# A vision tower with a mixture of experts on one core: the first steps in a new order of loads and set-up pieces, the first weight matrix with a semaphore of its own

## The reference

```python
gray = jnp.einsum('bchw,c->bhw', x, w)[:, None]
edges = conv(gray, scharr)                       # two 3x3 filters
edge = jnp.sqrt(jnp.square(edges)).sum(axis=1) / 2
h = concatenate([cls_tok row, edge rows])         # 257 rows
xn = layernorm(h)
u, v, q, k = split(silu(xn @ W1 + b1), 4)        # W1: 256 x 1024
attn = silu(q @ k.T per head) / S                # 16 heads of 16
h = h + (layernorm((attn @ v) * u) * gamma + beta) @ W2 + b2
h = h + ffn(layernorm(h))    # router: statistics, gelu, softmax, top 2 of 32
                             # experts with a capacity, 16 adjugates
```

## Time and profile before

| what | value |
|---|---|
| median of 3 runs | 1460.76 us |
| the profiled execution's own time | 1461.07 us |
| its span | 1459.2 us |
| TensorE busy | 1273.0 us, 87% |
| VectorE busy | 1212.3 us, 83% |
| ScalarE busy | 892.8 us, 61% |
| POOL busy | 482.5 us, 33% |
| mean granted TensorE clock | 0.932 of full speed |
| moved by DMA | 176.69 MB, mean 121 GB/s |

### The profile page before, as it was taken

How to read it: one execution, slowest core, us unless ns; L and a number is a source line. 1 busy time by engine, 2 the same in 40 slices (tenths; PEclk the granted TensorE clock), 3 DMA queues, 4 the chain that set the end, 5 groups by cost and what they waited for, 6 DMA issues and landing times. The chain is left out here.

```text
span 1459.2 us, 33138 instructions
## 1 busy us (share of the span) xinstructions
PE 1273.0 (87%) x11891; PEld 1025.1 (70%) x11891; DVE 1212.3 (83%) x3140; ACT 892.8 (61%) x1608; POOL 482.5 (33%) x457
## 2 busy tenths in 40 slices
PE   3699999999999999999973332499999999999996
PEld 2457667667667667667652232399999999999996
DVE  4589999999999999999879878877777777777773
ACT  1378878887887887887772352545555555555552
POOL 0022232233233233232213000235554545555543
PEclk9699999999999999999996555699999999999999
DMA  8535344345345445442040600055565665665652
GB/s 242 136 93 132 107 122 132 105 123 133 103 125 133 107 120 133 113 115 59 31 145 17 93 1 0 14 192 156 163 191 151 178 179 148 186 171 150 195 126 24
DMA packets 128185, 176.69 MB, mean 121 GB/s; under 512 B 19946, under 2 KB 116476, under 8 KB 123964
## 3 DMA queue, kind: packets, MB, share of 16 engines
q1 hardware_dynamic: 110652, 153.80, 35.6%
q0 software_dynamic: 17408, 21.25, 9.1%
HBM read 133.85 MB, written 41.15 MB: 120 GB/s over the span
## 5 line engine op out<-in xcount | busy, mean ns | idle before, releaser
L796 ACT ACTIVATE at<-ps_s 128x1024 f32<-128x1024 f32 x256 | 248.3, 1027 | 5.4 <-PE ps_s L532 4.3
L2368 POOL DMA_INDIRECT out_rows<-ye,slot_token x96 | 151.8, 1581 | 227.2 <-ACT ye L2213 213.5
L247 PE MATMUL ps_s<-xet,whi 128*128 128x322 f32 x640 | 206.1, 322 | 11.1 <-DVE wlo L2283 9.6
L249 PE MATMUL ps_s<-xet,whi 128*128 128x322 f32 x640 | 199.3, 311 | 0.0
L248 PE MATMUL ps_s<-xet,wlo 128*128 128x322 f32 x640 | 198.7, 310 | 0.0
L2182 ACT ACTIVATE sg<-ps_s 128x322 f32<-128x322 f32 x160 | 70.5, 440 | 172.5 <-PE ps_s L249 128.2
L2283 DVE TENSOR_TENSOR wlo<-raw,whi 128x640 fp32r<-128x640 f32 x192 | 153.9, 817 | 2.3 <-ACT whi L2192 1.3
L2266 DVE TENSOR_TENSOR hm<-ps_s,sg 128x322 f32<-128x322 f32 x128 | 63.2, 494 | 98.6 <-ACT sg L2182 77.6
L548 PE MATMUL ps_av<-at,uv 128*16 128x257 f32 x2048 | 136.8, 384 | 1.0 <-ACT at L840 0.5
L247 PEld LDWEIGHTS ps_s<-xet,whi 128*128 128x128 f32 x640 | 121.6, 190 | 19.3 <-issue 15.8
L247 PE MATMUL ps_av<-whi,hs 128*128 128x256 f32 (+1 forms) x480 | 134.5, 280 | 0.6 <-issue 0.3
(11 more groups left out here) (393 smaller groups left out, 3557.2 us busy)
## 6 DMA issues: line engine op xcount, KB each, us to landing
raw<-in_wexp SPq DMA_DIRECT2D x32, 1280.0 KB, 6.4
halo<-gray_dram SPq DMA_DIRECT2D x96, 288.0 KB
xb<-in_x SPq DMA_DIRECT2D x64, 384.0 KB, 4.8
raw<-in_wexp SPq DMA_DIRECT2D x32, 640.0 KB
gray_dram<-g SPq DMA_DIRECT2D x32, 256.0 KB, 3.5
out_rows<-h SPq DMA_DIRECT2D x64, 128.0 KB, 3.3
token_rows<-xf SPq DMA_DIRECT2D x64, 128.0 KB, 2.4
pre_dram<-pre SPq DMA_DIRECT2D x30, 128.0 KB, 1.7
```

Source lines behind the costliest of these rows:

```text
L247: nc.tensor.matmul(o, lh, rh, start=first, stop=False)
L249: return nc.tensor.matmul(o, lh, rl, start=False, stop=last)
L796: nc.scalar.activation(at[:, t, 2 * i:2 * i + 2, :, 0:R].rearrange("p j k q -> p (j k) q"), ps_s[i][:, :, :, :].rearrange("p j k q -> p (j ...
L2368: nc.gpsimd.indirect_dma_start(out=out, out_offset=bass.IndirectOffsetOnAxis(ap=slot_token[0:w, 3 * m + st:3 * m + st + 1], axis=0), in_=y ...
```

## The change

It touches the fill alone. SyncE's order is new: of the constants only the first 256 columns are loaded at the start (the rest, from the mask of the class values on, moves into the list of the later loads); the zeroing of `gray_dram` goes ahead of the taps and the class rows; W1 and b1qk follow, under the semaphore `w1_loaded`; then come the first gray's store, the pixels of image 1 and the first halo, and only then the other loads. On VectorE the cast of W1 becomes a piece of its own (`round_w1`), and the other pieces of the set-up move from step -2 into step -1, with the gray of image 2; the gray of image 3 goes to the end of step -1. TensorE and ScalarE follow with their own orders. The number of instructions stays the same but for one DMA.

```diff
--- before.py
+++ after.py
@@ -305,13 +305,14 @@
         fill = zeros[:, 0:3 * ROW].rearrange("p (n w) -> p n w", w=ROW)
         base_loaded, loaded, zeroed, filled, zero_set = (sem(n) for n in ("base_loaded", "loaded", "zeroed", "filled", "zero_set"))
         su_dve, su_act, su_pool, su_pe = sem("su_dve"), sem("su_act"), sem("su_pool"), sem("su_pe")
+        w1_loaded = sem("w1_loaded")
+        w1_group = [(w1f, w1.rearrange("(k p) n -> p k n", p=P)), (b1qk_sb[:, :], b1qk)]
         loads = [
-            (w1f, w1.rearrange("(k p) n -> p k n", p=P)), (gbf, gb), (b1qk_sb[:, :], b1qk),
-            (w2f, w2.rearrange("(k p) n -> p k n", p=P)), (r1f, r1w.rearrange("(k p) n -> p k n", p=P)), (r1mf, r1m), (b2f, b2),
+            (cst[:, CMV:NC_], consts[:, CMV:NC_]), (gbf, gb), (w2f, w2.rearrange("(k p) n -> p k n", p=P)), (r1f, r1w.rearrange("(k p) n -> p k n", p=P)), (r1mf, r1m), (b2f, b2),
             (b1uv_sb[:, :], b1uv), (r1b_c[:, :], r1b), (r2w_sb[:, :], r2w),
         ]
         LOADED = 16 * (len(loads) + 3)
-        S_BAND, S_VAR, S_CLSN, S_CLST, S_GAIN, S_W1, S_CW, S_W2, S_UVP, S_BIAS, S_R1, S_VC, S_ALL = 3, 6, 7, 8, 10, 11, 12, 14, 15, 16, 19, 22, 24
+        S_BAND, S_VAR, S_CLSN, S_CLST, S_W1, S_GAIN, S_CW, S_UVP, S_BIAS, S_W2, S_R1, S_VC, S_ALL = 3, 6, 7, 8, 10, 11, 12, 13, 14, 16, 19, 22, 24
 
 
         h0 = s1("h0", [P, 2, D])
@@ -660,7 +661,7 @@
 
             def class_row_qk():
                 pe.wait_ge(su_dve, S_CLST)
-                pe.wait_ge(loaded, LOADED)
+                pe.wait_ge(w1_loaded, 32)
                 for m in range(4):
                     for kt in range(2):
                         last = nc.tensor.matmul(ps_s[0][:, 0, 0, 32 * m:32 * m + 32], w1f[:, kt, 512 + 128 * m:640 + 128 * m],
@@ -692,16 +693,16 @@
                     conv(n, r, a, 0, "A0")
                     conv(n, r, a, 1, "A1")
                     class_row_uv()
-                    shift_rows()
-                    class_row_score()
                     return
                 if n == -1:
                     transposes(n, "B0", xn, xn_done, b + 1, xt_ps)
                     conv(n, r, a, 0, "A0")
                     pe.wait_ge(su_dve, S_W1)
                     proj_qk(n, b, 0, "B1")
+                    conv(n, r, a, 1, "A1")
+                    shift_rows()
+                    class_row_score()
                     proj_qk(n, b, 1, "B2")
-                    conv(n, r, a, 1, "A1")
                     proj_uv(n, b, 0, "B3")
                     proj_uv(n, b, 1, "B4")
                     pe.wait_ge(su_act, 3)
@@ -906,7 +907,7 @@
 
                 def class_row_silu():
                     act.wait_ge(su_pe, 2)
-                    act.wait_ge(loaded, LOADED)
+                    act.wait_ge(w1_loaded, 32)
                     for m in range(4):
                         last = nc.scalar.activation(qkcf[:, m, :], ps_s[0][:, 0, 0, 32 * m:32 * m + 32], ACT.Silu, bias=b1qk_sb[:, m:m + 1])
                     last.then_inc(su_act, 1)
@@ -927,20 +928,20 @@
                     class_row_silu()
                     abs_edges(0)
                     abs_edges(1)
-                    class_row_values()
-                    gray_red(act, gm)
-                    class_row_weight()
                     return
                 if n == -1:
                     turned_hi(xt, "B0", xt_ps, uv_ps, 2 * b, b, xt_hi)
                     abs_edges(0)
-                    gray_red(act, gm)
+                    gray_red(act, AHEAD)
                     silu_q()
                     hi_q()
+                    abs_edges(1)
+                    class_row_values()
                     silu_k()
-                    abs_edges(1)
+                    class_row_weight()
                     silu_uv(0)
                     silu_uv(1)
+                    gray_red(act, gm)
                     return
                 if n == 0:
                     act.wait_ge(su_dve, S_ALL)
@@ -1257,9 +1258,12 @@
                     dve.wait_ge(su_pool, 3)
                     slink(nc.vector.tensor_scalar(clsn, clsf, mv["z"][:, 0, 0:1], rs["z"][:, 0:1], ALU.subtract, ALU.mult), S_CLSN)
 
+                def round_w1():
+                    dve.wait_ge(w1_loaded, 32)
+                    slink(nc.vector.tensor_copy(w1s[:, 0, :, :], w1f))
+
                 def gains():
                     dve.wait_ge(loaded, LOADED)
-                    slink(nc.vector.tensor_copy(w1s[:, 0, :, :], w1f))
                     for kt in range(2):
                         nc.vector.scalar_tensor_tensor(r1f[:, kt, :], r1mf, 1.0 / D, r1f[:, kt, :], ALU.mult, ALU.add)
                         nc.vector.tensor_scalar(betaf[:, kt, :], ident, 0.0, gbf[:, 2 + kt:3 + kt], ALU.mult, ALU.add)
@@ -1325,38 +1329,39 @@
                     bands()
                     class_row()
                     class_row_turned()
-                    gains()
+                    round_w1()
                     gray_green(dve, 1)
                     gray_blue(dve, 1)
                     split_w1()
-                    class_weights()
                     edges(0)
                     edges(1)
                     stats_a()
+                    norm_a()
+                    return
+                if n == -1:
+                    turned_lo(xt, bank("B0")[:, :], xt_hi, b, xt_done)
+                    gains()
+                    class_weights()
+                    gray_green(dve, AHEAD)
+                    gray_blue(dve, AHEAD)
+                    double_q()
+                    class_values()
+                    split_q()
+                    biases()
+                    edges(0)
+                    double_k()
+                    biased(0)
+                    edges(1)
+                    stats_a()
+                    stack_k()
+                    norm_a()
+                    biased(1)
                     split_w2()
-                    norm_a()
-                    class_values()
+                    sum_weights()
+                    class_columns()
+                    class_kept()
                     gray_green(dve, gm)
                     gray_blue(dve, gm)
-                    return
-                if n == -1:
-                    biases()
-                    turned_lo(xt, bank("B0")[:, :], xt_hi, b, xt_done)
-                    edges(0)
-                    sum_weights()
-                    gray_green(dve, gm)
-                    double_q()
-                    gray_blue(dve, gm)
-                    split_q()
-                    double_k()
-                    edges(1)
-                    class_columns()
-                    stats_a()
-                    class_kept()
-                    norm_a()
-                    stack_k()
-                    biased(0)
-                    biased(1)
                     return
                 if n == NB:
                     nc.vector.tensor_copy(iota_b[:, :], cst[:, CIE:CIE + NE])
@@ -1655,20 +1660,22 @@
                     return
                 if n == -2:
                     load_x(sp, 0)
-                    sp.dma_start(cst[:, :], consts).then_inc(base_loaded, 16)
+                    sp.dma_start(cst[:, 0:CMV], consts[:, 0:CMV]).then_inc(base_loaded, 16)
+                    sp.wait_ge(zero_set, 1)
+                    sp.dma_start(gray_dram.rearrange("(p n) -> p n", p=P), zeros[:, :]).then_inc(zeroed, 16)
                     sp.dma_start(tapf, taps).then_inc(base_loaded, 16)
                     sp.dma_start(clsf, cls_rows).then_inc(base_loaded, 16)
-                    sp.wait_ge(zero_set, 1)
-                    sp.dma_start(gray_dram.rearrange("(p n) -> p n", p=P), zeros[:, :]).then_inc(zeroed, 16)
+                    for o, i in w1_group:
+                        sp.dma_start(o, i).then_inc(w1_loaded, 16)
+                    sp.wait_ge(zeroed, 16)
+                    store_gray(sp, 0)
+                    load_x(sp, 1)
+                    load_halo(sp, 0)
                     for o, i in loads:
                         sp.dma_start(o, i).then_inc(loaded, 16)
                     sp.wait_ge(su_pool, 1)
                     for k in range(3):
                         sp.dma_start(r1stf[32 * k:32 * k + 6, :], r1s).then_inc(loaded, 16)
-                    sp.wait_ge(zeroed, 16)
-                    store_gray(sp, 0)
-                    load_x(sp, 1)
-                    load_halo(sp, 0)
                     store_gray(sp, 1)
                     load_x(sp, 2)
                     load_halo(sp, 1)
```

## The result

The change makes the kernel slightly slower: 1464.48 us, median of 10 runs (1462.23 to 1465.95), against 1460.77 for the kernel before (1458.16 to 1461.89, 10 runs). The ratio is 1.0031 with a 95% interval of 1.0023 to 1.0039, so 3.7 us by the medians and 4.5 us by the ratio, just outside what can be told from no change. The profiled execution of the changed kernel, 1465.95 us, is the slowest of its ten.) The forecast was 1462.1, with no difference as the likeliest case.

The account below looks back on a forecast made before the run. VectorE's chain holds step 0 back, then image 4's late load: 0.7 us for that load plus 0.6 for the clock, +1.3 on the median 1460.76, gives 1462.1 us; range 1456.8 to 1465.5.

Parts of the forecast that it names:

- first convolution: TensorE's first convolution, behind the first halo: moves from 24.88 to 20.9 us, the halo coming 4.0 us earlier.
- second halo issued; landed: SyncE issues it at about 25.9 us (25.48 before); landing taken as 33.2, between bounds 31.9 and 34.0.
- xt ready: Step -1, the turned input of the q projection: ready at 30.7 us, before at 38.0.
- projection of step -1: TensorE's q projection of image 0, behind the second halo and half a convolution: 35.0 us against 38.12.
- shuffle of q: VectorE in step -1, after projection (2.9 us) and silu (0.9): begins at 38.9 us, before at 44.27.
- shuffle to the end of image 3's gray: VectorE's chain in step -1, lengthened by moved pieces: 19.8 us, so image 3's gray ends at 58.7.
- gray 4: Start of image 4's gray on ScalarE in step 0: 65.0 us against 64.30, a loss of 0.7.
- clock in step 0: TensorE's granted clock around step 0's projection: 1.3 us more at half pace, costing 0.6 us.
- The load of image 4: Pixels asked for only after image 3's gray; 6.3 us from there to image 4's gray, ScalarE waiting 3.9.
- Rival 1: Second halo doesn't gate; step -1's projection follows xt at 31.0 instead of 35.0 us: 1457.5 us, chance 0.30.
- Rival 2: TensorE stays cold through step 0, its clock taking 12.6 us to rise: 1465.4 us, chance 0.20.
- Rival 3: First halo comes no earlier; projection still at 35.0 and time 1462.1 us, not resting on it; chance 0.04.

Follow-up runs that it names:

- e3: Changed kernel with SyncE's later loads back ahead of the first gray's store; ratio 1.0014 to the kernel before.
- e1: Changed kernel with image 3's gray earlier in step -1 on ScalarE and VectorE; ratio 1.0001 to the kernel before.
- e8: Changed kernel with image 0's q projection ahead of image 1's first half convolution, ScalarE's pieces reordered to match; ratio 0.9985 to the kernel before.
- the repacked kernel: The kernel of e7, against which e9 tested the order of loads; 1454.56 us, ratio 0.9959 to the kernel before.
- e10: Changed kernel plus 18 unread TensorE products of 248 columns in the gap ahead of step 0's class turn; ratio 1.0016 to the kernel before.
- e5: Changed kernel plus 80 unread TensorE products of 64 columns ahead of step 0's class turn; ratio 1.0125 to the kernel before.
- e9: e7 with SyncE's later loads back ahead of the first gray's store; ratio 0.9991 to the kernel before.
- e7: Changed kernel with VectorE's wait filled, image 3's gray earlier, ScalarE's wait later, q projection ahead of the convolution; 1454.56 us, ratio 0.9959 to the kernel before.

## Why the forecast was nearly right, and where it fell short

It named the right place and mechanism, and its range held the time, but it gave no difference the best chance and was 2.4 us short (1462.1 for 1464.5). Two of its hits are partly luck, as said below. Its terms:

| term | forecast | measured |
|---|---|---|
| first convolution | 20.9 | 21.16 |
| second gray's store issued | 21.5 | 19.17 |
| second halo issued; landed | 25.9; 33.2 | 25.80; 33.82 |
| xt ready | 30.7 | 30.82 |
| projection of step -1 | 35.0 | 36.52 |
| shuffle of q | 38.9 | 40.35 |
| shuffle to the end of image 3's gray | 19.8 | 21.4 |
| from there to gray 4 | 6.3 | 5.9 |
| gray 4 | 65.0 | 67.65 |
| clock in step 0 | +0.6 | -0.8 |

- **The projection, 1.5 us too early.** The halo landed 0.6 later, within its bounds; the convolution took 1.94 for 1.8; and 0.76 us passed between convolution and projection, which the sum had left out. The profile names different releasers for that gap, or "issue", but the program and the traces settle it. The projection (unit B1) writes the PSUM bank that the convolution (A0) has just filled, and `bank_free` makes it wait until ScalarE's `abs_edges` has read the bank. ScalarE's rows, of the changed kernel and of e3:

```profile
35.83 0.60 ACT L804 ACTIVATE edge<-ps_f 128x512 f32<-128x512 f32 x1 [5.73 <-PE ps_f L468]
```

```profile
34.74 0.60 ACT L804 ACTIVATE edge<-ps_f 128x512 f32<-128x512 f32 x1 [0.77 <-PE ps_f L468]
```

  The edges end at 36.43 and 35.34, the projections start at 36.52 and 35.44. In all eight kernels with this order the projection starts 0.09 to 0.10 us after the end of the edges. In the kernel before, xt came 1.9 us after the edges' end (36.08 and 37.97), so this wait was hidden.
- **The halo's issue, right by luck.** SyncE got through the twelve loads in 5.4 us (13.79 to 19.17) where 7.4 had been taken, so the second gray's store went out 2.3 us earlier than the sum had it. Then that store took 6.6 us to land where the sum had 4.4. The two errors cancel to 0.1.
- **VectorE's chain, 1.6 us too short.** `norm_a`'s first half took 1.35 us (52.16) where it had taken 0.69. VectorE's row of the kernel before, and POOL's row of the changed kernel beside which the 1.35 us ran:

```profile
54.59 0.69 DVE L1045 TENSOR_SCALAR xn<-h,mva,rsa 128x256 f32<-128x256 f32 x1
```

```profile
51.45 1.92 POOL L1613 TENSOR_TENSOR h0b<-h,bias 128x512 f32<-128x512 f32 x1
```

  That is 0.66 us. The wait for h0b of image 0 was 1.22 for 0.9, the wait for `hi_q` 0.63 for 0.4; together 1.2 of the 1.6. POOL's h0b of this image took 1.25 us in the kernel before, and the same two pieces run side by side again in step 0 of the changed kernel. First POOL's row of the kernel before, then the two of step 0:

```profile
53.88 1.25 POOL L1608 TENSOR_TENSOR h0b<-h,bias 128x512 f32<-128x512 f32 x1
```

```profile
82.20 1.38 DVE L1046 TENSOR_SCALAR xn<-h,mva,rsa 128x256 f32<-128x256 f32 x1 [0.59 <-POOL rsa L1532]
```

```profile
82.13 1.29 POOL L1613 TENSOR_TENSOR h0b<-h,bias 128x512 f32<-128x512 f32 x1
```

  All twelve traces agree. With no h0b beside it the first half of `norm_a` takes 0.40 to 0.41 us. Beside one it ends some 0.15 us after h0b does: 0.69 where half a us of h0b was left, 1.35 to 1.38 where 1.2 us was. And this h0b took 1.91 to 1.93 us in the eleven kernels in which `stack_k` (50.96 above) runs beside its start, and 1.25 in the kernel before, in which it doesn't. The new order had put `stack_k` ahead of `norm_a`, and with it beside this h0b; the sum kept the old 0.69. That the engines held each other up is the reading of these rows; no run took POOL's piece away or put `stack_k` back.
- **The load of image 4.** Right in kind and nearly in size: the wait is 4.37 us where 3.9 was said, and e1 takes it away with the whole loss. The 3 us that were to be won at the start of step 0 did not appear at all (60.36 for the 57.2 forecast), as the chain before it was longer.
- **The clock had the wrong sign.** That hid part of the other errors: gray 4 was 2.65 us later than forecast, but the clock gave back 0.8 where the sum had added 0.6. Stretches of the changed kernel, columns as above:

```profile
72.00:72.50 0.50, 0.50 (x6) 0.15 (x8) 0.00 (x0) 0.20 (x1) 0.00 (x0) 0.50 0.82 262
72.50:73.00 0.50, 0.50 (x12) 0.24 (x8) 0.00 (x0) 0.50 (x2) 0.00 (x0) 0.88 1.04 320
```

  It rose at about 72.6, 3.3 us after the projection of step 0 began (69.33), where it took 4.9 before. From this step's class silu to the next is 21.75 us, against 22.5 before. So of the 3.35 us lost at gray 4, 2.6 were left at step 1's gray (89.15 against 86.56). After that little is added: the last class silu is 3.3 late, the median 3.7. Where this last 1.1 us comes from stays open.
- **Rival 1** did not occur, since the second halo gated just as was argued; e8 gives its price: 6.7 us against the changed kernel, where 4.0 was said, as the wait for the bank and the half clock of that projection went too. **Rival 2** fell: the clock came back in 3.3 us, not 12.6. **Rival 3** was wrong in its premise (the first halo did come 3.7 earlier), but its claim that the time does not rest on the first halo was borne out by e3, in which the time even fell.
- The chances were the weak point: the halo's path and the chain were taken with less waste between their pieces than there was, so both errors went the same way, and the chance of a loss over 0.2% was put at 0.21, with rival 2's clock as its main ground rather than these small sums.

## What to carry to other kernels

Where a buffer's next load waits for its last reader, the place of that reader in the program's order is the load's due time: moving the reader to the end of a step moved a wait of 6.8 us in one step to a wait of 4.4 us in the next, and behind more work. Before bringing a transfer forward, look at what stands behind the *next* one in each engine's order; here an early first halo cost 2.5 us while the projection stood behind the second, and was worth some 4 in the repacked kernel. Look as well at what a piece that moves to the front was hiding: the wait for the bank had been under a longer wait. And let a chain's forecast include the waits and small gaps between its pieces, which did not go down to zero here when it was repacked, and ask which pieces of another engine its pieces will now run beside.

## What the runs showed of the hardware

- 80 products of 64 columns, each with its own weight load, ran for 17.3 us with TensorE's granted clock at half (0.50), though matmul and weight load were both busy for the whole of 72 to 76 us. It rose between 84 and 88 us (0.70 in the mean), behind the projection's 256-column products. In e10, after 18 products of 248 columns (4.2 us), it rose between 68.0 and 68.5. The Trainium skill, "TensorE: Matmul & The Clock Gate", "Part 1: The HAM clock gate (the 'warmup' mystery)", has the clock follow how busy the engine has been; e10's rows agree with that, and e5's, as far as busy time in the profile goes, do not.
- An idle of 4.4 us ahead of the second halo's convolution left it at half clock (1.94 us for 16 products, projection 0.41 a product); with 0.27 us idle it ran at full (1.07, and 0.28). The length of the idle alone does not tell, though: after 1.50 us without work the projection of step -1 ran at half in e9 (0.41) and at full in e7 and e8 (0.28).
- In the first stretch the granted clock in the profile does not match the pace: it reads 1.00 from 10 to 28 us, but the first convolution takes 3.64 us for 32 products, where e7's next 32 (34.53) take 1.93 at 1.00.
- SyncE issued two loads of pixels in 2.62 us behind the twelve later loads (19.61), where it took 0.97 to 1.04 for them in the rest of the fill. But two others took 2.52 us with none of those loads near (94.00), so what makes such an issue slow stays open.
